# One core, two layers of attention and expert/quantized feed-forward: expert weights applied at the PSUM copy, gathers that add into x, a route split in two, norms six tiles ahead, one block

## The reference

```python
# LN = layer norm without weights
x = x + LN(x) + tril(ctx @ ctx.T) @ LN(x)            # attention of layer 0, no softmax
g = LN(x) @ gate.T                                   # 8 experts, the best 2 of each row
x = x + sum_k softmax(top2(g))[k] * expert_k(LN(x))  # silu(z W1) * (z W2), then W3; 256 -> 512 -> 256
x = x + softmax(LN(x) @ ctx.T / 16 + mask) @ ctx     # attention of layer 1
x = x + bitlinear(gelu(bitlinear(LN(x), w1, b1)), w2, b2)   # 8-bit rows, ternary weights, 256 -> 1024 -> 256
```

## Time and profile before

| | |
|---|---|
| median of 3 runs | 719.32 us (718.57 to 719.40) |
| the profiled execution, its own time | 723.95 us |
| its span, first to last instruction | 722.0 us |
| mean granted TensorE clock | 0.867 |
| PE busy | 563.3 us (78%) |
| DVE busy | 528.6 us (73%) |
| ACT busy | 368.1 us (51%) |
| POOL busy | 365.0 us (51%) |
| DMA | 74.80 MB, mean 104 GB/s |

### The profile page before, as it was taken

How to read it: one execution, slowest core, us unless ns; L and a number is a source line. 1 busy time by engine, 2 the same in 40 slices (tenths; PEclk the granted TensorE clock), 3 DMA queues, 4 the chain that set the end, 5 groups by cost and what they waited for, 6 DMA issues and landing times. The chain is left out here.

```text
span 722.0 us, 17429 instructions
## 1 busy us (share of the span) xinstructions
PE 563.3 (78%) x5923; PEld 487.9 (68%) x5923; DVE 528.6 (73%) x1494; ACT 368.1 (51%) x715; POOL 365.0 (51%) x387
## 2 busy tenths in 40 slices
PE   4687955009999999999999999505668747899996
PEld 3566844008999999999999999504545523565665
DVE  6887776805866766667655655239989997999997
ACT  2499743003343443443433443204676629999994
POOL 1015275779999999998000000177773226544440
PEclk9778755559999999999999999855667979999999
DMA  5998242422222222223222222294565200011112
GB/s 196 367 356 303 62 153 79 150 90 48 61 70 65 61 69 65 62 67 68 60 68 68 60 68 67 69 340 118 171 189 158 75 1 0 16 38 38 37 39 73
DMA packets 77588, 74.80 MB, mean 104 GB/s; under 512 B 44480, under 2 KB 67904, under 8 KB 76224
## 3 DMA queue, kind: packets, MB, share of 16 engines
q1 hardware_dynamic: 71360, 56.92, 25.4%
q0 software_dynamic: 6144, 16.79, 7.3%
HBM read 40.51 MB, written 23.86 MB: 89 GB/s over the span
## 5 line engine op out<-in xcount | busy, mean ns | idle before, releaser
L906 PE MATMUL banks<-z_turned,w_of_block 128*128 128x128 f16 x3408 | 203.7, 220 | 32.9 <-DMA z_turned<-z_rows 32.9
L906 PEld LDWEIGHTS banks<-z_turned,w_of_block 128*128 128x128 f16 x3408 | 191.8, 98 | 36.1 <-issue 33.0
L994 DVE SCALAR_TENSOR_TENSOR hidden_T<-banks,blk_inv,silu_T 128x512 f32<-128x512 f32 x71 | 53.3, 751 | 117.4 <-PE banks L906 95.8
L1192 POOL DMA_INDIRECT expert_rows_in<-expert_rows,places_of_rows x64 | 64.0, 999 | 144.0 <-POOLq L1023 125.0
L403 POOL DMA_INDIRECT z_rows<-z_parts,places_in_regions x64 | 64.5, 1008 | 88.8 <-DVE places_in_regions L716 70.5
L959 ACT ACTIVATE hidden_T_high<-hidden_T 128x512 fp32r<-128x512 f32 x71 | 44.9, 632 | 109.1 <-DVE hidden_T L994 109.1
L986 DVE COPY w_of_block<-w_parts 128x4096 f16 x71 | 94.2, 1328 | 3.9 <-issue 3.9
L919 PE MATMUL banks<-w_low,hidden_T_high 128*128 x284 | 85.8, 302 | 2.8 <-DVE hidden_T_low L1000 2.7
L952 ACT ACTIVATE silu_T<-banks,blk_inv 128x512 f32<-128x512 f32 x71 | 48.8, 688 | 67.0 <-PE banks L906 66.9
L919 PE MATMUL banks<-w_high,hidden_T_high 128*128 x284 | 79.6, 280 | 0.0
L919 PE MATMUL banks<-w_high,hidden_T_low 128*128 x284 | 79.3, 279 | 0.0
(11 more groups left out here) (240 smaller groups left out, 1307.7 us busy)
## 6 DMA issues: line engine op xcount, KB each, us to landing
expert_rows<-expert_out SPq DMA_DIRECT2D x71, 128.0 KB, 1.7
w_parts<-in_w SPq DMA_DIRECT2D x7, 1024.0 KB, 7.2
x_rows<-in_x SPq DMA_DIRECT2D x8, 512.0 KB, 6.2
c_T<-in_ctx_turned SPq DMA_DIRECT2D x16, 256.0 KB, 4.1
w_low<-in_w SPq DMA_DIRECT2D x8, 512.0 KB, 8.8
c_T_in<-in_ctx_turned SPq DMA_DIRECT2D x32, 128.0 KB, 2.3
c_in<-in_ctx_rows SPq DMA_DIRECT2D x32, 128.0 KB, 3.1
out<-rows_out SPq DMA_DIRECT2D x32, 128.0 KB, 1.7
```

The lines of the kernel that those rows point to most:

```text
L906: mm = pe.matmul(PS[:, 1 + half + 2 * u, hc * P:(hc + 1) * P], win[:, u, wp, c, at:at + P], zturn[:, j % ZB, k, :], start=(n == 0), stop=( ...
L994: v.scalar_tensor_tensor(out=g[:, :], in0=PS[:, 2 + 2 * u, :], scalar=blk_inv[:, j:j + 1], in1=s[:, :], op0=ALU.mult, op1=ALU.mult).then_i ...
L1192: pool.indirect_dma_start(rows[:, k, n, :], None, y_rows[:, :], bass.IndirectOffsetOnAxis(ap=place[:, R * i + k, n:n + 1], axis=0))\
```

## The change

1. A row that is scattered carries 8 bytes more: a code of the expert chosen first (c1) and exp of the gap between second and first logit. z_rows is declared as 258 32-bit words a row (1032 bytes). ACT makes the Exp of each route, DVE copies code and Exp behind put_down into the slots (told_put), and POOL's scatter waits for it.
2. SP loads code and Exp of a block's rows (load_told, eight blocks at a time); weigh() on DVE makes one weight a row from them, every eight blocks; keep_y applies it as ACT's scale. prob and its three instructions go. places() moves from ahead of hidden(0) to behind rest_g(0) and weigh(0).
3. Gathers add into x themselves (compute_op add): sum_rows, sum_rows2 and expert_rows_in go. The first gather of a tile is issued three tiles ahead of the second, which waits for it to land.
4. The route of tiles 8 to 15 becomes (8,12) and (12,16).
5. Layer 1: norms in 17 links, two Newton steps instead of three; moments of a tile six steps ahead of its first step (LEAD), the chain of links in two of four steps. Feed-forward norms in four sets of eight tiles, each begun within the attention; largest_x of tiles 0 to 7 and scale_x(0) in its last steps. The weights' passes on ACT stand in steps 16, 17 and 22 to 25.
6. b1's two parts are made as 128 x 8 and go through DRAM; two large memsets move from DVE to POOL; context loads wait for the gather of two tiles before; the weights load in quarters, one a tile, behind tile 8.
7. One block for the whole kernel: layer 1's engines wait for a count that POOL raises when all 71 blocks have left PSUM (steps_done), POOL also for the stores.
8. POOL's prepare scales with tensor_tensor; h_rounded has four buffers instead of two, and the last four tiles are rounded in one step.

```diff
+    z_rows = nc.dram_tensor("z_rows", (Z_ROWS, ZW // 2), I32, kind="Internal").ap()
...
-        ROUTES = ((0, 4), (4, 8), (8, 16), (16, 24), (24, 28), (28, 32))
+        ROUTES = ((0, 4), (4, 8), (8, 12), (12, 16), (16, 24), (24, 28), (28, 32))
...
+                    pool.wait_ge(told_put, pieces_done[route_of[t]])
...
+                def exp_gaps(r):
+                    t0, t1 = ROUTES[r]
+                    act.wait_ge(picked, PICK * (r + 1))
+                    a.activation(told[:, t0:t1, 1], dl[:, t0:t1], ACT.Exp).then_inc(exped, 1)
...
-                    ch.link(v.tensor_copy(put_at[:, tt, :], pos[:, tt, :]))
+                    ch.post(v.tensor_copy(put_at[:, tt, :], pos[:, tt, :]))
                     assert ch.n == PUT
+                    dve.wait_ge(exped, r + 1)
+                    for p0, p1 in pieces[r]:
+                        slots = slice(p0 % ZP, p0 % ZP + p1 - p0)
+                        v.tensor_copy(zp[:, slots, D:ZW // 2].bitcast(F32), told[:, p0:p1, :]).then_inc(told_put, 1)
 
...
+                def load_told(j):
+                    sp.dma_start(told_in[:, j, :], z_rows[bass.ds(rows[j], P), D:ZW // 2].bitcast(F32)).then_inc(told_got, 16)
...
+                    if j % READ == 0:
+
+                        after(sp, weighed, WEIGH * (j // READ))
+                        for n in range(j, min(j + READ, NB)):
+                            load_told(n)
...
-                        ch.link(pool.tensor_scalar(raw[:, cols], raw[:, cols], wsc[:, e:e + 1], None, ALU.mult))
+                        ch.link(pool.tensor_tensor(raw[:, cols], raw[:, cols], wsc[:, e:e + 1].broadcast_to([P, H]), ALU.mult))
...
-                    a.activation(ye[:, u, :], PS[:, 6 + u, 0:D], ACT.Copy).then_inc(ye_made, 1)
+                    a.activation(ye[:, u, :], PS[:, 6 + u, 0:D], ACT.Copy, scale=weight[:, j:j + 1]).then_inc(ye_made, 1)
...
+                def weigh(b):
+                    cols = slice(READ * b, min(READ * b + READ, NB))
+                    n = cols.stop - cols.start
+                    ch = Chain(dve, weighed, WEIGH * b)
+                    dve.wait_ge(told_got, 16 * cols.stop)
+                    ch.post(v.tensor_tensor(hit[:, 0:n], told_in[:, cols, 0], blk_code[:, cols], ALU.is_equal))
+                    ch.link(v.tensor_scalar(share[:, 0:n], told_in[:, cols, 1], 1.0, None, ALU.add))
+                    ch.post(v.reciprocal(share[:, 0:n], share[:, 0:n]))
+                    ch.link(v.tensor_tensor(hit[:, 0:n], hit[:, 0:n], told_in[:, cols, 1], ALU.max))
+                    ch.link(v.tensor_tensor(weight[:, cols], hit[:, 0:n], share[:, 0:n], ALU.mult))
+                    assert ch.n == WEIGH
...
-                later[0]()
                 hidden(0, 0)
                 hold(2, 0)
                 rest_g(0, 0)
+                weigh(0)
+                later[0]()
...
+                def load(t):
+
+                    after(sp, o_made, t - (R - 1))
+                    sp.dma_start(cTs[:, t % R, :], ctd[:, t:t + 1, :]).then_inc(c_in[t % R], 16)
+                    sp.dma_start(cs[:, t % R, :], cd[:, t:t + 1, :]).then_inc(c_in[t % R], 16)
...
+                    load(t)
+                    if t < 2 * R:
+                        load_w(t // 4 % 2, t % 4)
...
+                def gather(t, n):
+                    after(pool, r_in[t % R], 32 * (t // R) + 16 * n if n else 0)
+                    pool.indirect_dma_start(X1[:, t, :], None, y_rows[:, :],
+                                            bass.IndirectOffsetOnAxis(ap=place[:, t, n:n + 1], axis=0),
+                                            compute_op=ALU.add).then_inc(r_in[t % R], 16)
...
+                for t in range(T):
+                    if t + LAG < T:
+                        gather(t + LAG, 0)
+                    gather(t, 1)
+                    if t == R:
+                        pool.memset(b3[:, :].bitcast(F32), 0.0).then_inc(magic_made, 1)
+                        pool.memset(ialT[:, :, :].bitcast(F32), 0.0).then_inc(magic_made, 1)
...
-                def sum_rows(i, k):
+                def moments_x(i, k):
                     dve.wait_ge(r_in[k], 32 * (i + 1))
...
-                def sum_rows2(i, k):
-                    dve.wait_ge(x2_half, R * i + (k + 1))
-                    v.scalar_tensor_tensor(out=x_row(i, k), in0=rows[:, k, 1, :], scalar=prob[:, 1, at(i, k)],
-                                           in1=x_row(i, k), op0=ALU.mult, op1=ALU.add).then_inc(x2_made, 1)
...
-                def front(i, half):
-                    for k in range(half * Q, (half + 1) * Q):
-                        sum_rows(i, k)
-                        if k % Q >= 1:
-                            sum_rows2(i, k - 1)
-                    sum_rows2(i, half * Q + Q - 1)
-                    for k in range(half * Q, (half + 1) * Q):
-                        moments_x(i, k)
...
+                        s = R * i + k
+                        chain = coming[(s + 3) // Q] if s % Q in (1, 2) and s < T - Q else iter(())
+                        f = normed[0 if s < 21 else 1 if s < 29 else 2] if s >= 13 else iter(())
+                        if s % Q == 1:
+                            at_tile(moments_x, i, k, -LEAD)
+                            advance(chain, 1)
                         at_tile(masked, i, k, 1)
-                        advance(chain, 1)
-                        if m >= 1:
-                            at_tile(sum_rows2, i, k, 1 - R)
-                            advance(chain, 1)
+                        advance(chain, 3)
+                        if s % Q == 3:
+                            advance(f, 2)
                         at_tile(add_out, i, k, 4)
-                        advance(chain, 1)
+                        advance(chain, 2)
+                        if s % Q in (0, 3):
+                            advance(f, 2)
                         at_tile(invert, i, k, 3)
-                        advance(chain, 1)
+                        advance(chain, 2)
                         at_tile(moments_x3, i, k, 5)
-                        advance(chain, 1 if m < 3 else LINKS)
-                        at_tile(sum_rows, i, k, -R)
-                        if i == 0 and k == R - 1:
-                            b1_parts()
-                        if m == 3:
-                            at_tile(sum_rows2, i, k, -R)
-                            for n in range(k - 3, k + 1):
-                                at_tile(moments_x, i, n, -R)
-
+                        if s % Q != 1:
+                            at_tile(moments_x, i, k, -LEAD)
+                        advance(chain, LINKS if s % Q == 2 else 1)
+                        advance(f, NORM_N if s in (20, 28, T + Q) else 1 if s % Q in (0, 3) else 0)
+                        if s == 21:
+                            for n in range(2):
+                                mean_of(n)
+                        if s == 22:
+                            dve.wait_ge(scales_made, 4)
+                            v.tensor_scalar(wmore[:, :], wmean[:, :], LOW_STEP / 127.0, None, ALU.mult).then_inc(scales_made, 1)
+                        if T - Q <= s < T + Q:
+                            largest_x(s - (T - Q))
+                        if T <= s < T + Q:
+                            advance(first_x, 2)
...
+                    for t in ([s - 5] if 0 <= s - 5 < T - Q else range(T - Q, T) if s == T + 1 else ()):
+                        round_h(t)
+                    advance(normed[3], 2 if s < 12 else NORM_N)
```

416 lines of the change are left out of this document (221 added, 195 removed).

## The result

The changed kernel takes 758.75 us (median of 4 runs, 755.20 to 761.89), the kernel before, measured beside it, 719.36 (4 runs, 718.57 to 723.85): ratio 1.0533, 95% interval 1.0469 to 1.0596. It is 5.3% slower where 2.4% faster was forecast. The profiled execution took 761.89 us with a span of 760.1.

The account below looks back on a forecast made before the run. PE was taken to bound the experts, DVE the second attention before, POOL after. Terms -3.7 + 2 - 9 - 6.3 = -17 gave 705.0 from the profiled 722.0, 702.3 against the median; range 690 to 720, chance 0.78 to 0.8.

Parts of the forecast that it names:

- What bounds: Whole kernel: PE bounds the experts, DVE the second attention before; without the sums POOL's gathers, 2.5 us a tile, bound it.
- The adding gather: Second attention: an adding gather costs POOL 0.95 us, like a plain one; by the skill's rule landing might lengthen 3.1 us.
- over 1.3 us apart: Second attention, sign of being wrong: adding gathers stand further apart than this, where 1.25 us was forecast.
- Rival A: Second attention: adding gathers at double price, 2.2 us each, 755 us in all; slower than before from 1.6 us; chance 0.10.
- A landing up to about 6.5 us costs POOL nothing: Second attention: a tile's second gather waits for its first, issued six gathers or 7.5 us earlier, so such landings stay hidden.
- Layer 0: Layer 0: splitting the route of tiles 8 to 15 removes three slot waits; -3.7 us, bounds -8 and +2.
- Start of the experts: First expert blocks: SP's code loads are hidden, but places() and weigh() delay down(1); +2 us, bounds 0 and +4.
- The experts' run: Remaining expert blocks: later weigh() calls, code loads and POOL's new scaling stay hidden; zero, bounds -1 and +3.
- Rival E: Expert stage: slower by split loads or longer row pitch, ending slower than before beyond 15 us; chance 0.03 for that.
- Second attention beside the price: Second attention: first gather at 465.6, last add_out at 578.5 instead of 587.45; gain 9, the boundary's 0.7 in it.
- Head and loop: Feed-forward: last add_out to first gelu takes 4 us, gain 6.3, bounds 3 and 8; the DVE-bound loop behind it 0.
- The roundings: End of the feed-forward: the last four roundings done together save no instruction; 0, bounds -2 and +1.

Follow-up runs that it names:

- g_plain: The changed kernel with its 64 gathers plain, overwriting x's rows instead of adding to them: 728.94 us, ratio 1.0113.
- m_head: m_best with the eight largest_x and the first feed-forward scaling back behind the last add_out: 722.42 us, ratio 1.0008 against the kernel before.
- b_again: The kernel before, unchanged, run again for a trace on the same chip: 721.88 us.
- b_adding: The kernel before with the last 48 of its 64 gathers adding to their buffer instead of overwriting it: 740.94 us, ratio 1.0265.
- e_ahead: The changed kernel with the loads of codes, except the first group, issued two at a time and a group ahead: 757.52 us, ratio 1.0518.
- e_scalar: The changed kernel with GpSimd's scaling back to tensor_scalar, as in the kernel before: 771.44 us, on the slower chip.
- m_route: m_best with tiles 8 to 15 ranked in one route again: 722.06 us, ratio 1.0025 against the kernel before.
- m_best2: The kernel of m_best run once more, on a chip like the first: 717.98 us, ratio 0.9951 against the kernel before.
- m_best: The changed kernel with plain gathers, DVE weighing and adding, no codes, earlier places(), old scaling and roundings: 747.31 us, ratio 0.9829, slower chip.
- t_tail: The changed kernel with the last four feed-forward roundings done one a step, as in the kernel before: 773.93 us, on the slower chip.

## Why the prediction was wrong, step by step

**What bounds.** Right: DVE in before's second attention, POOL once the sums are gone. POOL's stream in before already ended only at 548.9, 1.8 us behind my own forecast of 547.1 for after. DVE and POOL were nearly level there, so taking work from DVE alone could win little between first and last gather.

**The adding gather: the step that failed.** "I take 0.95, since POOL writes a list of the same 128 rows." An adding gather brings 96 more packets and holds POOL 0.59 us longer, with half the bytes too. The mark that the prediction set for being wrong, "over 1.3 us apart", is passed by half a microsecond. 63 x 0.59 = 37 us; g_plain gives 35.8 us of stage back. Rival A was this mechanism, at 2.2 us instead of 1.84, with a turning point of 1.6 us, and had 0.10. It gave 755 for 758.75, by luck, with errors against each other: its price was 0.36 us a gather too high, 23 us in all, while the first gather came 9.8 us later than in its sum (473.7 against 465.6 less 1.7), it put 24 us behind the last gather's start where 34.4 were needed, and nothing for the 4.9 us at the end. (Its landing at 611 also leaves out the doubled busy time: 606.9 + 1.9 + 3.1 is 611.9.) The row of the plain gather could not show the price; the fault was to lean on it where the time hung on it by 38 us.

By the Trainium skill (DMA: Bandwidth & Descriptors, Rules for kernel authors) an accumulating DMA reads its destination and writes it later. The landings agree with it in sign: 3.6 us plain, 4.2 adding, in otherwise equal kernels. I read from that rule a price in landing only, 3 us; it was 0.6, and nearly all of the loss was paid on the issuing engine.

"A landing up to about 6.5 us costs POOL nothing" was read from the middle of the stream. The last tile's first gather stands only four gathers ahead of its second, 5 us at the price taken, which leaves room for a landing of 4 us. It cost nothing here: at 1.84 us a gather the room is wider, and no gather waited in g_plain either.

**Layer 0.** Right, as a mechanism. Tile 8's first scatter is at 79.84 (forecast 79.5), tile 16's at 110.18 (110 to 111), the last at 151.47 (152), the first block at 157.99 (158.5). ACT waits for a slot of z_parts twice (5.0 us) where it did five times (8.7). Over all profiles but the slower chip's, the first expert matmul stands at 158.1 on average with the split (ten profiles, 155.9 to 160.0) and at 161.0 without it (four, 159.4 to 162.1): 2.9 us, a little under the 3.7 forecast and within the bounds.

**Start of the experts.** +2 forecast, 4.9 measured. The delay of down(1) was foreseen (PE waited 1.61 us for it). "PE waits for DVE's first hidden_T_low until 170.5 anyway, so that is hidden" was wrong: down(0) stands behind up(1) in PE's order, and hidden_T_low(0) was ready at 166.6; PE was held by SP's loads. I had taken an instant of before for a fixed one, though the same change moved it four microseconds forward.

**The experts' run.** Zero with bounds -1 and +3; 6.6 us measured. Loads, weigh() and the wait for it seem to be most of it: without them down(1) to down(69) falls from 290.3 to 285.1 us (before 283.9). How much of that is SP's eight loads in a row (4.5 us in one pair of profiles) and how much the new scaling beside DVE costs (2.3 in another) isn't known better than the 6 us by which the stage scatters. DVE is in the changed kernel between 175 and 200 us idle 3.1 us before hidden_T, 6.4 in before: "DVE's third of idle time" is no third while POOL prepares. On the scaling the Trainium skill (GPSIMD Engine Reference, Specifications) has a rule that my working left out: GpSimd's SBUF interfaces are shared with VectorE, with contention for DVE instructions with two SBUF inputs. hidden_T_low has two, and agrees: 0.68 us at its shortest, 1.00 on average beside the new form and 0.76 beside the old. Rival E had 0.03 beyond 15 us; its size was near. It named the separate loads, which the runs make likely, and the longer row pitch, which the kernels with all taken back rule out: they keep it and run their experts in 301 us.

**Second attention beside the price.** With plain gathers 117.1 us where my sum has 112.9 (465.6 to 578.5). The gathers' stream was right, 81.0 us against 81.5. Behind the last gather's start it took 36.1 instead of 31.4 us. DVE is busy 31.8 of these 36.1 us (30.2 of 34.4 in the changed kernel): ten steps at 1.93 us were too cheap. That largest_x and the feed-forward norms in them are the reason fits m_head, whose stage is 5.1 us shorter without largest_x.

**Head and loop.** The head was right (4.4 us, forecast 4). But by m_head a head moved into a stage where DVE is the bound is worth 1.5 us, not 6; it is worth its price only where DVE waits for POOL. "The loop has the same instructions a tile, DVE bound: 0" was 1.5 us off up to the last gelu, with PE's granted clock at 0.79 in the first 14 us against 0.98 in before. No run tested the clock, but the traces agree on it: in six of the 18 profiles (before, b_again, b_adding, e_ahead, e_scalar, m_route) it is 0.97 to 0.99 there and first to last gelu takes 105.8 or 105.9 us; in the other twelve it is 0.79 to 0.82 and takes 107.1 to 107.5. Kernels that differ nowhere in these instructions are on both sides. The first 14 us of the changed kernel, then of e_ahead:

```profile
631.00:645.00 14.00, 9.47 (x40) 4.51 (x39) 9.01 (x25) 11.90 (x20) 6.30 (x12) 0.79 0.00 0
```

```profile
624.30:638.30 14.00, 8.95 (x48) 4.69 (x47) 9.97 (x27) 13.19 (x22) 7.40 (x13) 0.98 0.00 0
```

The roundings, "0, bounds -2 and +1", cost 3.4.

**Signs.** Even at 0.95 us a gather the forecast would have been on the wrong side (g_plain 1.0113). The small terms had bounds that were narrow and mostly centred on nothing; together they lost 16 us where I had +1.3.

**Open.** The kernels with all taken back run 301.3 us from first matmul to first gather, 2.7 less than before with the same instructions a block. It lies in PE's own busy time (295.5 us in m_best2, 298.1 in before), not in its waits; the cause stays open. Why the slower chip took 6% more wasn't settled either, and a profile of the kernel before is missing there. The longer stages on it are layer 0 and the second attention (139.6 us in m_best, 126.5 in m_best2), while the experts are alike (300.6 and 301.1).

## What to carry to other kernels

An operation that the trace doesn't show and that stands in a row of 64 on one engine isn't to be priced by its nearest relative; the forecast has to say what follows at twice the price, and weigh that by how little is known, not by how plausible the relative is. Before work is moved off an engine, look at which engine is next: here POOL ended its stream within 2 us of what DVE allowed. Work that is hidden by a pause needs that pause to exist after the change too, and waits queued ahead of what feeds the bound engine (SP's small loads, a link on DVE, a copy on ACT) can reach it. A stage's length from one profile is worth no more than its scatter between profiles of the same code: here 0.3 us in one kernel and 6 us in another.

## What the runs showed of the hardware

- A gather that adds to its destination holds GpSimd 1.54 us for 128 rows, a plain one 0.95, with rows of 1024 bytes; with 512 bytes the adding one takes 1.541 us too. Each adding one brings 96 more packets to the software queue. The landing grows from 3.6 to 4.2 us at the median.
- A `tensor_tensor` with a broadcast operand on GpSimd is quicker than `tensor_scalar` (1.53 against 2.25 us for 128x512), and a DVE instruction with two SBUF inputs is slower beside it (hidden_T_low, mean 1.00 against 0.76 us in t_tail and e_scalar).
- The same code of the feed-forward runs 1.5 us longer when PE's granted clock is about 0.8 in its first 14 us than when it is 0.98 (18 profiles, no exception).
